# A graph network kernel: the search for row blocks by comparisons and one-hot products in place of one round of gathers, the first node stage among the remaining gathers, and one piece of the one-hots made on ScalarE

## The reference, cut to what matters

```python
for l in range(3):
    f1 = relu(x[row] @ nb_W[l] + nb_b[l]); f2 = relu(x[col] @ self_W[l] + self_b[l])
    h = relu(concat([f1, f2], axis=1) @ att1_W[l] + att1_b[l])
    log_alpha = (h @ att2_W[l] + att2_b[l])[:, 0]
    mask = clip(sigmoid(log_alpha) * (ZETA - GAMMA) + GAMMA, 0.0, 1.0)
    rowsum = segment_sum(mask, row) + 1e-06
    d = clip(rowsum ** -0.5, 0.0, 10.0)
    x = segment_sum((mask * d[row] * d[col])[:, None] * x[col], row)
    out = out + x
x = layernorm(x0 + out)
x = layernorm(x + relu(segment_sum(w * x[col], row) @ weight + bias))   # w: 1/sqrt(degree) of both ends
```

## Time and profile before

| | us |
|---|---|
| median of three runs | 10558.67 |
| the profiled execution | 10557.76 |
| its span, first to last instruction | 10555.8 |
| sort ends, search begins | at 915.6 |
| first gather of round two | at 945.7 |
| first gather of the keys | at 1214.4 |
| first instruction of the node stage | at 1402.9 |
| first one-hot of the edge stage | at 1514.8 |
| busy, whole span: PE, DVE, ACT, POOL | 80%, 77%, 26%, 43% |

### The profile page before, as it was taken

One profiled execution on the slowest core, in us unless ns is written; L12 is line 12 of the kernel. 1 busy time (PEld: TensorE's weight loads), 2 busy tenths in 40 slices (PEclk: granted clock), 3 DMA queues, 4 the chain that ended last, 5 costly groups with the idle time before them and its releaser, 6 DMA issues. The chain is left out here.

```text
span 10555.8 us, 718911 instructions
## 1 busy us (share of the span) xinstructions
PE 8414.4 (80%) x288474; PEld 7547.9 (72%) x288474; DVE 8176.5 (77%) x13852; ACT 2744.8 (26%) x5816; POOL 4535.6 (43%) x4893
## 2 busy tenths in 40 slices
PE   0110048888887999979998999979999899969996
PEld 0110037777776888869998888869999788858885
DVE  9995068888888777777777777767777777787775
ACT  0110024444443333310000333310000333323332
POOL 0003711111111888711111888811111788858883
PEclk9755579999998999999999999989999999989997
DMA  1000137777775555557776555547776555545552
GB/s 26 0 0 16 19 100 223 222 223 222 220 222 184 160 161 161 140 157 212 212 213 191 160 161 159 156 138 212 212 212 200 155 161 160 160 115 161 159 161 72
DMA packets 1006558, 1635.93 MB, mean 155 GB/s; under 512 B 260806, under 2 KB 745388, under 8 KB 1005996
## 3 DMA queue, kind: packets, MB, share of 16 engines
q1 hardware_dynamic: 952200, 1581.31, 50.8%
q0 software_dynamic: 54272, 53.46, 2.5%
HBM read 1348.02 MB, written 286.27 MB: 155 GB/s over the span
## 5 line engine op out<-in xcount | busy, mean ns | idle before, releaser
L911 PE MATMUL bank<-tab,extra 128*64 128x64 bf16 x201684 | 3986.5, 197 | 439.3 <-DVEq L1410 180.7
L911 PEld LDWEIGHTS bank<-tab,extra 128*64 128x64 fp8e4 x201684 | 3565.3, 112 | 928.9 <-issue 870.1
L689 POOL TENSOR_TENSOR planes<-planes 128x448 f32<-128x448 f32 (+1 forms) x2744 | 2614.5, 965 | 556.9 <-DVE planes L1573 501.6
L621 POOL DMA_INDIRECT xg<-q_table,ixb x588 | 648.2, 1102 | 3668.2 <-ACT ixb L761 3423.1
L1009 PE MATMUL bank<-planes,extra 128*128 128x192 bf16 x19992 | 2100.1, 247 | 42.1 <-POOL planes L689 11.2
L797 ACT CAST bank<-planes 128x448 f32<-128x448 bf16 (+1 forms) x2744 | 1514.9, 552 | 2357.0 <-DVE planes L1566 2351.0
L1566 DVE TENSOR_TENSOR planes<-bank,mask_all 128x448 f32<-128x448 f32 (+2 forms) x2744 | 1699.2, 619 | 226.0 <-PE bank L911 144.6
L1573 DVE TENSOR_TENSOR planes<-planes,bank 128x448 f32<-128x448 f32 (+1 forms) x2744 | 1726.2, 629 | 126.6 <-ACT bank L797 126.6
L1445 DVE SCALAR_TENSOR_TENSOR extra<-bank,a2w 128x448 f32<-128x448 f32 (+1 forms) x2058 | 1299.4, 639 | 579.1 <-PE bank L934 509.0
L1009 PEld LDWEIGHTS bank<-planes,extra 128*128 128x128 fp8e4 x19992 | 1586.7, 96 | 174.8 <-issue 40.6
L934 PE MATMUL bank<-plb,extra 128*128 128x64 bf16 x44982 | 1606.7, 194 | 6.7 <-issue 6.6
(11 more groups left out here) (217 smaller groups left out, 4302.2 us busy)
## 6 DMA issues: line engine op xcount, KB each, us to landing
extra<-one_hots SPq DMA_DIRECT2D x1372, 368.0 KB, 3.2
extra<-one_hots SPq DMA_DIRECT2D x2156, 224.0 KB, 3.6
extra<-one_hots SPq DMA_DIRECT2D x588, 192.0 KB, 2.4
one_hots<-extra SPq DMA_DIRECT2D x490, 224.0 KB, 2.0
one_hots<-extra SPq DMA_DIRECT2D x294, 368.0 KB, 3.0
work<-slot_rows_cols SPq DMA_DIRECT2D x196, 368.0 KB, 4.6
work<-slot_rows_cols SPq DMA_DIRECT2D x294, 224.0 KB, 4.0
work<-slot_rows_cols SPq DMA_DIRECT2D x98, 192.0 KB
```

Of the source, the lines that this page charges most:

```text
L621: nc.gpsimd.indirect_dma_start(out=to, out_offset=None, in_=table_d, in_offset=bass.IndirectOffsetOnAxis(ap=index, axis=0)).then_inc(done, 16)
L689: nc.gpsimd.tensor_tensor(tiles(yrl[:, 2, a * C:b * C]), tiles(yrl[:, 1, a * C:b * C]), upper[:, 1, a:b, :], ALU.subtract).then_inc(low_re ...
L911: mm = pe.matmul(bank[half * S:(half + 1) * S, i * C:(i + 1) * C], oct_[:, k * P + half * S:k * P + (half + 1) * S], tab[:, at:at + C], st ...
```

## The change

1. **Round two without gathers.** The table `run_samples`, its store and its 99 gathers go, and so does round one. GpSimd writes all boundaries to all lanes (98 iotas of 128 x 99) once the last turn of the sort is copied. VectorE marks, for each boundary, the lane that holds it (`lane_before` < boundary <= last key of this lane; a DMA fetches the last key of the lane before), in four chunks (`ROUND2`: 28, 28, 28, 15 boundaries), and TensorE multiplies these marks by `g2x` (64 samples of each lane, and the number of the lane's first run); VectorE counts from PSUM.
2. **The first node stage between the rounds.** VectorE runs the node stage in four parts around the comparisons of round three (`level3`) and ahead of the work on the key bytes, and makes the `xs` copies itself. TensorE and ScalarE have their node stage ahead of what they did before it. SP stores P and Q before the bytes.
3. **Bytes in parts.** `start` is released chunk by chunk; key bytes are made and stored in four parts (33, 33 and 32 column blocks, the extra pieces), each when its gathers are in. `planes_of` follows at once, ahead of the slow setup. The first six broadcasts (`numbers`) are issued ahead of it as well.
4. **One piece on ScalarE.** `ort` 2 is made by two activations, Abs(byte - lane) and ReLU(1 - that), between the sigmoid and the turned copies.

```diff
 # gpsimd
-            for i, cs in enumerate(CHUNKS):
-                for c in cs:
-                    gather(L2[:, c * C:(c + 1) * C], g2_d, runs_i[:, c:c + 1], level2_in[i])
+            pool.wait_ge(turned, len(SORT_T) * 16)
+            for rb in range(NB):
+                op = nc.gpsimd.iota(bounds.bitcast(I32).rearrange("p (c r) -> p c r", r=NB)[:, :, rb], [[1 << 14, NC1]],
+                                    base=KEY_BIT + (rb << 21), channel_multiplier=0)
+            op.then_inc(bounds_ready, 1)
             pool.wait_ge(sorted_out, 16)
             for i, cs in enumerate(CHUNKS):
-                pool.wait_ge(run2_ready, i + 1)
...
-            pool.wait_ge(start_ready, 1)
+                pool.wait_ge(run2_ready, 2 + i)
+                for j, c in enumerate(cs):
+                    gather(slots[i][:, j * C:(j + 1) * C], sorted_d, run2_i[:, c:c + 1], level3_in[i])
+            for i, cs in enumerate(CHUNKS):
+                pool.wait_ge(start_ready, i + 1)
                 for c in cs:
+                    if c < NB:
+                        gather(keys[:, c * S:(c + 1) * S], sorted_flat, start_i[:, c:c + 1], keys_in[i])
 # sync
+            sp.dma_start(lane_before[1:P, :], A[0][0:P - 1, F - 1:F]).then_inc(before_in, 16)
             sp.dma_start(sorted_d.rearrange("(p r) c -> p (r c)", p=P), A[0]).then_inc(sorted_out, 16)
...
+            planes_out(0)
+            for i, (a, b) in enumerate(LO_PARTS):
+                sp.wait_ge(lo_ready, i + 1)
+                sp.dma_start(lo_d[:, a // 4:b // 4], lo8.bitcast(I32)[:, a // 4:b // 4]).then_inc(lo_out, 16)
...
+            sp.wait_ge(lo_out, LO_STORES * 16)
+            sp.wait_ge(pq_out, 32)
+            sp.wait_ge(tab_ready, 1)
+            for kind in KINDS:
+                numbers(0, kind)
             sp.wait_ge(ctl_ready, 1)
 # scalar
+                def last_one_hots(R, late):
+                    lo, hi = piece(LAST_MADE)
+                    if late:
+                        wait_alone(act, last_made, value(act, R))
+                    wait_alone(act, rb_in[LAST_MADE], value(act, R * 16 + 16))
+                    nc.scalar.activation(apart, rb[:, lo:hi], ACT.Abs, bias=minus_p[:, 0:1]).then_inc(apart_ready, 1)
+                    if late:
+                        wait_alone(act, turn_one_hots, value(act, R * NT))
+                        wait_alone(act, made_out[LAST_MADE], value(act, R * 16))
+                    wait_alone(act, apart_ready, value(act, R + 1))
+                    nc.scalar.activation(oh1[:, lo:hi], apart, ACT.Relu, bias=1.0, scale=-1.0,
+                                         saturate=False).then_inc(last_made, 1)
...
                     if late:
                         sigmoid(value(act, n - 1))
                     if first:
+                        last_one_hots(R, late)
                         turned_one_hots(t)
 # tensor
+            for i, cs in enumerate(ROUND2):
+                pe.wait_ge(run_found, i + 1)
+                if i >= 2:
+                    pe.wait_ge(round2_used, i - 1)
+                for j, c in enumerate(cs):
+                    at = j % 7 * (C + 1)
+                    mm = pe.matmul(banks[4 * (i % 2) + j // 7][0:NB, at:at + C + 1], bounds[:, c * NB:(c + 1) * NB], g2x,
+                                   start=True, stop=True)
+                mm.then_inc(round2_ps, 1)
 # vector
+            for i, cs in enumerate(ROUND2):
+                a, b = cs[0] * NB, (cs[-1] + 1) * NB
...
+                st.done(v.tensor_scalar(above[i % 2][:, 0:b - a], bounds[:, a:b], lane_before[:, 0:1], None, ALU.is_gt))
+                st.wait(dve)
+                v.scalar_tensor_tensor(bounds[:, a:b], bounds[:, a:b], A[0][:, F - 1:F], above[i % 2][:, 0:b - a], ALU.is_le,
+                                       ALU.mult).then_inc(run_found, 1)
+            def round2(i):
...
+                for c, n, rows in given:
+                    st.done(v.tensor_tensor(held[:, c - cs[0]:c - cs[0] + n, :], rows[:, :, 0:C],
+                                            thr[:, c:c + n].unsqueeze(2).to_broadcast([NB, n, C]), ALU.is_lt))
+                st.wait(dve)
+                st.done(v.tensor_reduce(cnt[:, cs[0]:cs[-1] + 1], held, AX_X, ALU.add))
...
+                v.tensor_copy(run2_i[:, cs[0]:cs[-1] + 1], run2[:, cs[0]:cs[-1] + 1]).then_inc(run2_ready, 1)
+            layer_weights(0)
+            nodes_of(0, True, range(0, 2))
+            level3(0)
+            nodes_of(0, True, range(2, 3))
+            level3(1)
+            nodes_of(0, True, range(3, 4))
+            level3(2)
...
             pieces(st)
             dve.sem_inc(pos_ready, 1)
+            nodes_of(0, True, range(4, NCH // 2))
+            wait_alone(dve, plane_steps, NCH * 4)
+            dve.sem_inc(q_ready, 1)
...
-            dve.wait_ge(keys_in, (NB + XP) * 16)
...
+            for i, (a, b) in enumerate(LO_PARTS[:-1]):
+                ca, cb = a // S, b // S
+                dve.wait_ge(keys_in[i], (cb - ca) * 16)
+                st.done(v.tensor_scalar(lo_i[:, a:b], keys_i[:, a:b], 14, None, sh_r))
...
             dve.sem_inc(lo_ready, 1)
+            ns0 = Steps(nv, 0)
+            planes_of(ns0, work[:, 0:NB * C], resid_p)
             dve.wait_ge(xcolT_ps, 1)
...
-                    make(("ort", 2), R, (turn_one_hots, value(dve, R * NT)) if late else None)
```

More of the change, by code:

```diff
@@ L477, in block_of_rows @@
                             store_or(value(sp, R - 1), (("oct", 1), ("ort", 0), ("oct", 2)).index(kind))
-                for kind in KINDS:
-                    numbers(0, kind)
                 block_of_rows(0, False, False)
@@ L564, in layer @@
             def layer(l, first):
[L565 to L567 removed]
+                if not first:
+                    planes_out(l)
                 wait_alone(sp, pq_out, l * 32 + 32)
@@ L806, in layer @@
             def layer(l, first):
[L807 to L817 removed]
+                if not first:
+                    node_stage(l)
                 wait_alone(act, q_ready, l + 1)
@@ new lines, in _, with per_node, planes_of @@
+            for i in range(len(ROUND2)):
+                round2(i)
+            def per_node(a):
+                return a.unsqueeze(2).to_broadcast([P, NB, C])
+            def planes_of(ns, given, resid):
+                to = [tab[:, pl * NB * C:(pl + 1) * NB * C] for pl in range(NPL)]
+                ns.done(v.tensor_copy(to[0], given))
+                ns.wait(dve)
+                ns.done(v.tensor_tensor(resid, given, to[0], ALU.subtract))
+                ns.wait(dve)
+                ns.done(v.tensor_copy(to[1], resid))
+                ns.wait(dve)
+                ns.done(v.tensor_tensor(to[2], resid, to[1], ALU.subtract))
+                ns.wait(dve)
+                dve.sem_inc(tab_ready, 1)
@@ L1648, in layer @@
-                wait_alone(dve, plane_steps, (l + 1) * (NCH * 4))
-                dve.sem_inc(q_ready, 1)
-                planes_of(ns, work[:, 0:NB * C], resid_p)
+                ns = ns0 if first else Steps(nv, l * NODE_STEPS)
+                if not first:
+                    layer_weights(l)
+                    nodes_of(l, False, range(NCH // 2))
+                    wait_alone(dve, plane_steps, (l + 1) * (NCH * 4))
+                    dve.sem_inc(q_ready, 1)
+                    planes_of(ns, work[:, 0:NB * C], resid_p)
```

389 lines of the change are left out of this document (204 added, 185 removed).

## The result

| | before | after |
|---|---|---|
| median of 4 runs each, us | 10558.35 | 10236.95 |
| lowest to highest | 10556.5 to 10561.17 | 10232.02 to 10238.84 |
| profiled execution, its span | 10557.76, 10555.8 | 10238.56, 10236.8 |
| sort ends | 915.6 | 917.0 |
| first gather of round three | 1076.3 | 949.4 |

The ratio is 0.9695, 95% interval [0.9678, 0.9711]: 321 us less, against a forecast of 290.

The account below looks back on a forecast made before the run. Bound by serial pieces up to 1514.8 us, then by one block's lateness in the edge stage. 245 + 1.1 + 44 = 290 us off 10557.8 gives 10267.7, forecast 10268, range 10228 to 10318.

Parts of the forecast that it names:

- Step 1: Round two replaced by marks and products: first gather at 945.7, so 130.6 us gone; bounds 3 us less or 18 more.
- Step 2: Gathers of round three and keys without a break, 1.275 us each, 17 us of stalls by VectorE; last lands at 1215.1.
- Step 3: Node stage hidden under the gathers: 14 to 18 us a pair, over by 1147, 45 us of cover to spare.
- Step 4: Key bytes: only the last part and extra pieces, 13.3 us, stay behind the last gather; done at 1228.4.
- Step 5: Planes (20.3 us) and slow setup (20.6, plus 0.4 for the copy) follow; first one-hot at 1269.7, 245 us earlier.
- Step 6: One piece to ScalarE in 97 edge blocks: 0.45 us of TensorE's 0.85 us wait for the sums' copy go, 44 us.
- table load: Rival, chance 0.05: Abs and Sigmoid need different tables, two loads of 1.28 us per edge block; 10428.
- Iotas: Rival, chance 0.08: GpSimd's iotas are held by the sort's comparisons and start at 915.6; 17.5 us more, 10286.
- starving: Rival, chance 0.12: VectorE's casts and copies hold the gathers too, stalls about 50 us in place of 17; 10301.
- the slower case: Rival, chance 0.02: two activations overrun ScalarE's room in the edge stage; at 8.5 us 78 us more, 10636.

Follow-up runs that it names:

- the node stage alone: The changed kernel with layer 1's node stage in one piece behind the last keys, which puts the first two byte parts there too: 10372.0 us, ratio 0.9835.
- the early copy: The changed kernel with the copy of the row sums moved ahead of the second group's hidden values on VectorE: 10151.92 us, ratio 0.9627.
- the held ones: The changed kernel with GpSimd's 98 iotas held until the sort has ended: 10255.58 us, ratio 0.972.
- wait filled: The changed kernel with 6 useless products of 128 columns in TensorE's wait for the row sums' copy: 10219.99 us, ratio 0.9688.

## Why the prediction was right, and where it wasn't

**What bounds the kernel**: serial pieces up to the first one-hot, then one block's lateness. Both held; the node stage alone (131 us) and the early copy (89 us) show either kind. But "1797.2 us for 98 blocks, 18.34 us each" was a misreading: the window ended 60 us too early, and the average block of the whole stage is 18.80.

**Step 1** (first gather at 945.7; 949.4). The sort ended 1.4 us later, which is no more than two traces of one kernel differ by (914.3 and 917.0), and TensorE made VectorE wait 2.1. The mechanism was right; the mis-sized term is the f32 product: 0.336 us, at granted clock 0.5, where I had 0.12 to 0.24 by columns from 7 transposes of 128 columns. Each comes as two records of 0.168, so a product of 65 columns isn't half of one of 128. Two sums of the step were also off by little: 915.7 + 2.5 is 918.2 and not 918.7, and the marks add up to 16.0 us and not 16.3. The iotas cost nothing, as the held ones (18.3 us alone, 18.8 beside the sort) confirm.

**Step 2** (17 us of stalls; 22.0 up to the 197th gather). The mis-sized term is the byte parts: 14.1 us and not 6. I let six of eight gathers through, but a scalar step in SBUF behind a two-input step holds the gather further, to its own end. Node stage and round three took 7.9 where I had 11. That gathers are held is what the Trainium skill (SBUF — State Buffer, the box on DVE blocking SWDGE) warns of, and it spoke against this change. The box itself is about operations in the mode that takes both ports; two inputs in SBUF stand in the list above it, and there only against a GpSimd operation that reads SBUF, a condition that step 2 left out. The rows show gathers held by both kinds of step. In amount they cost 22 us, and the work put under the gathers gained 131 with these stalls paid.

**Step 3**: pairs of 17.5 to 18 us, the stage over at 1143.6 where 1147 stood. **Step 4**: 13.6 us for 13.3. **Step 5**: planes 20.3 as forecast, slow setup with the copy behind it 19.1 for 21.0. First one-hot 238 us earlier in place of 245: the 7 us are 3.7 of step 1 and 5.0 of step 2, less 1.6 of steps 4 and 5.

**Step 6**: 0.46 us a block for 0.45, and yet the step named the wrong wait. It said "0.45 of these 0.85 us go"; none did. The masks came 0.45 us earlier, which took the 0.3 us ahead of the row sums; TensorE then ran earlier, too, and came to the same wait as much earlier as VectorE did. Both engines had been shifted by one cause; this is read from the two traces and from the version with the piece back on VectorE, where the fourth wait returns and the third stays. The question to put to the trace of before was what TensorE waits for first behind the masks: the row with 0.31 us, which the prediction left out and the profile puts down to "issue". Ending on the right number here was luck in part: with the wait I named, the bounds were 0 and 82.

**The surplus of 31 us.** -7 at the first one-hot, +1 by the block's size, **+21 by the clock**, +16 behind the edge stage. The clock: 38 stretches at 0.5 (1.2 GHz) in the edge stage before, 147 us in all, and 23 after, 79 us; a block with a single one is 1.0 to 1.2 us longer. The prediction had no term for it, since it multiplied what an undisturbed block gains by 97; the whole stage, at 18.80 us a block against 18.34 undisturbed, would have shown that 45 us lay outside such blocks. On the chips of this kind the stretches go with TensorE's waiting. The table has its idle time from 2000 to 2400, some 22 blocks:

| | TensorE idle, us | stretches at 0.5 |
|---|---|---|
| before | 50.4 | 38 |
| last one-hots on VectorE | 50.4 | 36 |
| changed kernel, two traces | 44.4 | 23, 24 |
| wait filled | 38.5 | 1 |
| sums' copy early | 29.6 | 1 |

On the slower chip the order is another: 53.3 us with 40 stretches, 50.9 with 42, 49.9 with 95, 44.7 with 56. So "less waiting, fewer stretches" is shown for chips of the first kind alone, and what makes the clock fall stays open. Behind the edge stage the kernel before takes 7183 us in its one trace, and nine traces of the changed kernel and its versions on such chips take 7166 to 7172. Of the 16 us between the first two traces, 10 lie between layer 1's last copy of the row sums and layer 2's first, 2 or 3 in layer 2's 98 blocks, the rest behind them. No experiment was made on them, and they stay open.

**The rivals.** No table load stands in the edge stage, with Abs and Relu beside Sigmoid, as the Trainium skill (ScalarE: Activation LUTs, section Table sets: the hidden batching unit) had it. The two activations take 1.77 and 1.70 us, 3.56 with their gap, where I had 3.7. Iotas, starving and the slower case didn't come. The sentence that all values it names lie at 10230 to 10428 leaves out its own slower case, 10636.

## What to carry to other kernels

A stage that is written anew to fit under another engine's work may take 1.7 times as long and still be hidden whole; price it by the cover, then subtract the stalls it causes. Cut a stage's window where its last block ends, and compare the average block with the undisturbed one: the difference is a cost that no single block's timeline shows. Before crediting a step with shortening a wait, follow both sides: if one cause delays the waiter and the one waited for, removing it leaves the wait as it is, and the gain is elsewhere. The wait that stays may be the better target: moving one copy of 0.15 us by two steps gave 89 us, 27 of them by the clock. On a slower chip the same move left the blocks as they were, so a gain of this kind belongs to the chip on which it was measured.

## What the runs showed of the hardware

- A wait of 0.83 us a block on TensorE, cut to 0.5 by 6 products without use, took the stretches at granted clock 0.5 from 24 to 1 and 21 us off the kernel. On the slower chip 8 such products, where that wait was 0.2 us, took them from 40 to 95.
- 98 iotas of GpSimd into SBUF take 18.8 us beside VectorE's two-input comparisons and 18.3 alone; an indirect gather beside such operations and scalar steps in SBUF takes up to 3.38 us in place of 0.97, and one that started under a two-input step ends 0.84 us behind it, or, where a scalar step follows at once, 0.11 us behind that.
- A float32 product of 65 columns takes 0.336 us in two records at granted clock 0.5.
- Of two chips on which the kernel before takes 10545 and 11324 us, the slower one has idles of TensorE that no row explains (1.3 us a block), and a version that gains 89 us on the one leaves the blocks of the other as long as they were.
